# Cross-attention with a routed feed-forward on one core: where a slot's transposes and its block product stand in the order

## The reference

```python
q  = layernorm(x) @ Wq + bq                  # 16 heads of 16
k, v = split(ctx_1024 @ Wkv + bkv)
attn = softmax(q k^T / 4)                    # per head, 128 x 128
x1 = x + (attn v) @ Wo + bo
n  = layernorm(x1)
scores = n @ w_router                        # keep the 96 highest of 128 rows
x2 = x1 + where(kept, gelu(n @ w_block), n)
```

## Time and profile before

| what | us |
|---|---|
| median of three runs | 903.74 |
| the profiled execution | 904.1 |
| its span, first to last instruction | 902.3 |
| PE busy / PEld (weight loads) busy | 864.8 (96%) / 718.8 (80%) |
| DVE busy | 857.9 (95%) |
| ACT busy | 870.6 (96%) |
| POOL busy | 789.6 (88%) |
| granted TensorE clock, mean | 0.991 |

### The profile page before, as it was taken

The page is one execution under the profiler, slowest core; times in us unless marked ns, Lnnn a source line. Parts: engine busy times, 40 slices in busy tenths (PEclk is TensorE's granted clock), DMA queues, the critical chain, the costliest instruction groups (busy, mean ns, idle before and its releaser), DMA issues. The chain is left out here.

```text
span 902.3 us, 30174 instructions
## 1 busy us (share of the span) xinstructions
PE 864.8 (96%) x9842; PEld 718.8 (80%) x9842; DVE 857.9 (95%) x2068; ACT 870.6 (96%) x4632; POOL 789.6 (88%) x1489
## 2 busy tenths in 40 slices
PE   6999999999999999999999999999999999999972
PEld 6778888888888888888888888888888888888752
DVE  5888999999999999999999999999999999999987
ACT  4999999999999999999999999999999999999984
POOL 5468879999999999999999999999999999998865
PEclk9999999999999999999999999999999999999997
DMA  7221123232323232223333222323222323211102
GB/s 233 69 65 53 54 63 86 79 93 59 84 82 89 72 96 69 79 79 85 84 83 91 57 80 88 91 72 95 61 85 79 87 78 90 75 40 40 41 24 94
DMA packets 71357, 70.40 MB, mean 78 GB/s; under 512 B 12064, under 2 KB 63520, under 8 KB 71200
## 3 DMA queue, kind: packets, MB, share of 16 engines
q1 hardware_dynamic: 69840, 67.68, 26.4%
q10 hardware_dynamic: 1360, 0.79, 0.3%
HBM read 35.13 MB, written 16.78 MB: 58 GB/s over the span
## 5 line engine op out<-in xcount | busy, mean ns | idle before, releaser
L646 ACT ACTIVATE e_sb<-ps_s,neg_max 128x128 f32<-128x128 f32 x2048 | 772.1, 639 | 2.8 <-DVE neg_max L805 2.7
L646 ACT ACTIVATION_READ_ACCUMULATOR e_sb<-ps_s,neg_max 128x1 f32 x2048 | 718.2, 464 | 0.0
L805 DVE TENSOR_REDUCE neg_max<-ps_s 128x4 f32<-128x512 f32 x512 | 331.0, 666 | 19.7 <-PE ps_s L385 18.2
L385 PE MATMUL ps_s<-q_eo,k_sb 32*128 32x256 f32 x2048 | 146.6, 399 | 3.6 <-ACT e_sb L646 1.5
L450 PE MATMUL ps_a<-e_sb,v_pad 128*32 128x128 f32 x4096 | 138.4, 276 | 1.5 <-POOL v_pad L1168 0.9
L344 PE MATMUL ps_a<-w_o_sb,o_sb 128*128 128x256 f32 x512 | 131.7, 379 | 4.0 <-DVE v_sb L929 3.8
L450 PEld LDWEIGHTS ps_a<-e_sb,v_pad 128*32 128x32 f32 x4096 | 104.1, 109 | 23.2 <-issue 21.5
L385 PEld LDWEIGHTS ps_s<-q_eo,k_sb 32*128 32x128 f32 x2048 | 95.8, 184 | 32.9 <-issue 28.7
L344 PEld LDWEIGHTS ps_a<-w_o_sb,o_sb 128*128 128x128 f32 x512 | 93.8, 189 | 22.8 <-issue 4.7
L1157 POOL TENSOR_TENSOR x_sb<-x_sb,bo_sb 128x256 f32<-128x256 f32 x128 | 105.1, 822 | 0.2
L1168 POOL TENSOR_TENSOR v_pad<-v_sb,recip 128x256 f32<-128x256 f32 x128 | 79.5, 621 | 29.1 <-DVE recip L865 27.1
(11 more groups left out here) (113 smaller groups left out, 2213.8 us busy)
## 6 DMA issues: line engine op xcount, KB each, us to landing
x_sb<-in_x SPq DMA_DIRECT2D x64, 256.0 KB, 3.0
c_sb<-in_ctx SPq DMA_DIRECT2D x64, 256.0 KB, 3.0
out<-z_sb SPq DMA_DIRECT2D x64, 256.0 KB, 2.4
q_eo<-q_raw SPq DMA_DIRECT2D x504, 32.0 KB, 2.0
z_sb<-in_L_xattn_Wkv ACTq DMA_DIRECT2D x2, 256.0 KB, 6.7
z_sb<-in_L_xattn_Wq ACTq DMA_DIRECT2D x1, 256.0 KB, 3.6
w_z_sb<-in_L_ffn_w_block SPq DMA_DIRECT2D x1, 256.0 KB, 8.0
w_o_sb<-in_L_xattn_Wo SPq DMA_DIRECT2D x1, 256.0 KB, 7.1
```

The costliest lines, as they stand in the source:

```text
L385: mm = nc.tensor.matmul(ps_s[:, bank(b, j), c, :, :], k_sb[rows, r2, c, h * T:(h + 1) * T], q_eo[rows, r2, :, c, h, :], start=True, stop=True)
L646: last = nc.scalar.activation(e_sb[:, b % 3, j, c, par, :], ps_s[:, bank(b, j), c, par, :], ACT.Exp, bias=neg_max[:, b % 4, h:h + 1], accu ...
L805: nc.vector.tensor_reduce(neg_max[:, b % 4, :].rearrange("p (c j q) -> p j c q", c=C, j=J)[:, j, :, :], ps_s[:, bank(b, j), :, :, :], AX.X ...
```

## The change

On TensorE, from slot 4 on, the transposes of block s+8 stand ahead of the scores of block s instead of behind them, with the same wait. On VectorE, `product_scaled(s-4)` stands directly behind `inverse_sums_23(s)`, ahead of `final(s-16)` and the statistics, and it always waits for `rstd2_ready`. In the start-up: the queries of the pair 6 come behind the attention of block 1 instead of ahead of it (the block product between does nothing in that slot); on SP the load of x's pair 14 moves behind the first scatter of queries, the loads of ctx's pairs 12 and 14 move behind the second scatter, and a wait for the value weights stands ahead of the load of ctx's pair 8; on GpSimd the memset of the second half of `q_eo` moves behind the bias of x of block 1.

```diff
@@ SP @@
             load_x(12)
-            load_x(14)
+            sp.wait_ge(w_in["v"], 16)
             load_c(8)
             load_c(10)
             queries_even_odd_of_pair(2)
+            load_x(14)
+            queries_even_odd_of_pair(4)
             load_c(12)
+            load_x(16)
             load_c(14)
-            queries_even_odd_of_pair(4)
-            load_x(16)
             queries_even_odd_of_pair(6)
@@ TensorE @@
             for s in range(2, B - 1):
                 sure = 20 <= s < B - 8
+                if s >= 4:
+                    transpose_inputs(s + LEAD, s > 4)
                 scores(s)
                 if s < 4:
                     transpose_inputs(2 * s + 4)
-                else:
-                    transpose_inputs(s + LEAD, s > 4)
                 values(s - 1)
@@
                 if s < 4:
                     transpose_inputs(2 * s + 5)
-                if s == 2:
-                    queries_or_keys_of_pair(6, 0)
                 if s >= 4:
                     inputs_ready(s + LEAD + 1)
                 block_product(s - 4, sure)
@@
                 attention(s - 1, sure)
+                if s == 2:
+                    queries_or_keys_of_pair(6, 0)
@@ VectorE @@
                 inverse_sums_23(s)
+                product_scaled(s - 4)
                 final(s - 16, sure)
                 stats2_of_pair(s - 3)
                 if s >= 4:
                     stats1_of_pair(s + 12)
-                product_scaled(s - 4, sure)
@@ GpSimd @@
-            nc.gpsimd.memset(q_eo[:, 1, :, :, :, :], 0.0).then_inc(q_eo_zero, 1)
...
             input_and_bias(0)
             input_and_bias(1)
+            nc.gpsimd.memset(q_eo[:, 1, :, :, :, :], 0.0).then_inc(q_eo_zero, 1)
```

## The result

The changed kernel took **943.25 us** (median of 4 runs, 943.06 to 943.82) against 903.99 (4 runs, 903.71 to 904.31): 1.0435 times as long, 95% interval 1.0417 to 1.0453. The prediction was 942 us, range 922 to 956, slower. The profiled execution took 943.25 us with a span of 941.5, so the spans differ by 941.5 - 902.3 = 39.2 us. The lines of the code that the steps name are one number higher here than before (scores L386, transposes L415, maxima L806, inverse sums L859, product L942, final L995).

What follows compares the result with a forecast made beforehand. The prediction took a newly closed loop through VectorE's product and TensorE's transposes to bound the kernel, 6.86 us per plain slot against 6.67. 904.1 plus 37.9 (steady part), 1.0 (queries) and -0.4 (slot 119) gave 942 us, range 922 to 956.

Steps and rivals of the forecast that it cites:

- the loop: Slots 5 to 119: scores, VectorE's chain, product, transposes, next scores close a loop of 6.86 us per plain slot; chance 0.90.
- The step that was off: TensorE's slot: attention, projection and the rest come earlier, then wait for the product, so they are covered and add nothing.
- the sign that the transposes start about 0.05 us behind the product's end: Steady slots: if right, transposes wait for the product in nearly every slot and start about 0.05 us after it.
- TensorE's idle time grow to about 5% of a slot: Steady slots: TensorE idles about 5% of a slot; nothing charged, as the clock stayed at 1.00 in the drain.
- The rule against my 0.56: Transposes' start to scores' start, taken as 0.56 us; weight loads pulled ahead would make it 0.15 us per slot lower.
- Queries of pair 6: Start-up: queries behind attention 1 delay VectorE's inverse sums and scores(3) by 1.0 us, bounds 0 and 1.03.
- The loads and the memset: Start-up: moved x and ctx loads, the value-weights wait and GpSimd's memset cost nothing.
- The end: Slot 119 to 120: no transposes ahead of the scores, slot falls to about 6.29, -0.4 us; drain unchanged.
- The forecast of 38.5: Whole kernel: 37.9 us for the steady part, 1.0 for the queries, -0.4 for slot 119.
- (a): Rival, faster: transposes get a free place if inverse sums come 5.5 us or less after their scores; 895 us, chance 0.05.
- (b): Rival, no change: ScalarE is full at 6.67 us and every other shift vanishes in slack; 904 us, chance 0.05.
- (c): Rival, milder: scores follow transposes after 0.41 us and the start-up move is hidden; 924 us, kept inside the forecast.

Runs made afterwards that it cites:

- the run with both moves: The changed kernel with the product moved again, ahead of maxima 0, and keys and queries emptied ahead of maxima 1: 937.16 us, ratio 1.0365.
- the first experiment: The kernel before with only the transposes moved ahead of the scores, the product left behind final and statistics: 1072.17 us (one run).

## Why the prediction was right, point by point

**The mechanism.** TensorE issues in order, and with the transposes ahead of the scores, the scores wait for whatever VectorE hands to TensorE late in the slot before. That closed a loop that had been open. The product's part of it is shown: with the product late a plain slot grew to 7.87 (7.83 by the loop), with the transposes back behind the scores the loss was gone.

**The terms of the loop**, forecast and measured (the middle values of slots 36 to 115, the time from the product to the transposes from the slots where the product ends last): scores to maxima 3, 1.28 and 1.29; maxima 3 to inverse sums, 4.40 and 4.39; to the product 0.11 and 0.11; the product 0.46 and 0.43; to the transposes 0.05 and 0.05; transposes to scores 0.56 and 0.59 (609.95 - 609.36, and 624.25 - 623.66). Sum 6.86 both times. The slots with s % 8 = 4 were forecast at 7.27 and took 7.25, those with 5 to 7 at 7.06 and took 7.05. Those with 0 were forecast at 7.16 and took 7.18, but that agreement is luck: the residual's path ended last there, not the product's loop, whose terms add up to 7.13. Final, statistics and x1_low did vanish in VectorE's wait for the scores, even where a final took 0.89 us.

**The step that was off** is "Attention, projection and the rest of TensorE's slot come earlier [...] and then wait for the product, so they are covered". They are not covered in plain slots. With the transposes out from behind the scores, TensorE reaches the transposes of x1 before VectorE has emptied the keys or queries from their bank, and that path is 0.06 longer than the product's: 1.30 from scores to maxima 3, 3.53 from there to the end of the emptying (607.86 - 604.33), 0.15 to the transposes of x1, 0.34 to attention, 1.01 to the transposes, 0.59 to the scores, together 6.92. In 47 plain slots 0.056 is 2.6 us, and the steady part came out 2.3 above the forecast (809.0 against 806.7). So the sign that the transposes start about 0.05 us behind the product's end holds only in the 55 slots with s % 8 = 4 to 7 and router steps; in the others it is 0.09 to 0.11. Nor did TensorE's idle time grow to about 5% of a slot: by its records it was busy 6.92 of 6.92 us in slot 83.

**Inside TensorE's path** lies a cost that I had put down as a delay only: the order of the groups of matmuls. From the last start of one group to the first start of the next it was, before, 0.20 from attention to scores, 0.30 from scores to transposes and 0.03 from transposes to values, together 0.53. After, it is 0.20 from attention to transposes, 0.20 from transposes to scores and 0.30 from scores to values, together 0.70. With 0.02 more inside the values TensorE's own slot thereby grows by about 0.19, from 6.57 (what the slots with s % 8 = 2 took before, with TensorE waiting for nothing) to an estimated 6.76 (6.86 in the run with both moves, less the 0.10 of waiting). This is above ScalarE's 6.69, so if that figure holds, no rearrangement of VectorE's work alone could bring the slot back to what it was before.

**The rule against my 0.56**, of the Trainium skill (TensorE: Matmul & The Clock Gate, The mechanism), was that weight loads for row strips that don't conflict are pulled ahead. The row gave 0.59, above my figure, so no part of that gain was there. The weights of the scores were loaded at 609.95, with the first matmul, while the last transpose had started at 609.75:

```profile
609.95 0.74 PEld L386 LDWEIGHTS ps_s<-q_eo,k_sb 32*128 32x128 f32 x16 [0.17 <-issue]
```

Nor is it clear that the rule speaks of this step at all: the transposes are 128*128 in their rows and so take every row strip, those of the scores among them. Another rule of the Trainium skill bears on this better: TensorEngine Tiling (Array Packing), Key Properties, says that a change of tiling mode drains TensorE. The trace agrees: 0.20 us lie between the last start in one mode and the first in the next (transposes of x1 to attention, attention to transposes, transposes to scores), and 0.30 from scores to values, against 0.03 to 0.12 where both groups use the full array and are short.

**The first slots.** Queries of pair 6: forecast 1.0, measured 1.2, above my upper bound of 1.03. The bound took attention's time alone, from its first matmul to the next; what it missed is the 0.2 us that attention adds where it splits transposes and queries, two groups that use the full array. The loads and the memset cost nothing, as forecast. **The end:** slot 119 fell by 0.34 us (6.33 against 6.67; forecast 0.4), and the drain is the same within 0.1.

**The sum.** Between the two profiled executions: 40.1 for the steady part, +1.25 from scores 0 to scores 4, -0.3 for slot 119, +0.1 behind it, and -1.9 for the clock ahead of scores 0: 39.2, as the spans say. The forecast of 38.5 is this close partly by luck: it had the steady part 2.3 us too low and the start 0.2, while the clock of the one execution of before that was profiled took 1.9 away.

**The rivals.** (a) needed the inverse sums 5.5 us behind their scores; they came at 5.68. (b) fell with the loop of 6.86, and (c) with the 0.59 and with the 1.2 of the start.

## What to carry to other kernels

Before moving a step forward on an engine that works in order, list everything that engine must receive between the step's new place and the same place one round later, and close the loop for each. A list of waits names what came last, not what it cost: of the 32.9 us that it put down to the product before, only 3.7 went away when the product came 5 us earlier, and even those were worth nothing. When two paths come out within 0.1 us of each other, taking one away shows only the next: three different results of VectorE's one chain (keys, product, residual) took turns here. A step that comes to stand between two groups of one array mode, or out from between them, changes what the switches of mode cost in every round, even when the work is the same; here that is about 0.19 us a slot.

## What was not expected of the hardware

The granted clock ahead of scores 0 differs between executions of one and the same code (0.57 and 1.00 from 11.2 to 15.2 us in two profiles of before). Scores 0 start 2.3 us apart in these two, and up to 2.6 apart over all twelve profiles, more than the 1.2 that the start-up edits make; such edits are judged from scores 0 on. And the final, one and the same instruction, took from 0.46 to 0.91 us within the run after:

```profile
L995 DVE SCALAR_TENSOR_TENSOR z_sb<-z_sb,half_keep,x_sb x128: 461/480/906, 137.7 to 938.3; 128x256 f32<-128x256 f32 x128
```

These are least, median and most in ns, from the view of that line. No run here tells why; where it stood in the loop, in the first experiment, it cost 0.4 us more in each slot with s % 8 = 5 to 7.
